# Planned durations of DMAs and of one VectorE add in a list-scheduled attention and int8 layer

## The chip, the cores and the metric

The kernel runs on the 8 cores of one Trainium2 chip. Each core takes two of the 16 sequences and works alone; nothing is exchanged between cores. The metric is the device time of the slowest core, in microseconds (us), lower is better.

## The reference, cut to what matters

```python
x = x + LN(attn(LN(x)))           # x: 16 x 2048 x 1024, f32
x = x + LN(ffn(LN(x)))

# attn: 16 heads of 64, decay linear attention
q = elu(x @ Wq) + 1;  k = elu(x @ Wk) + 1;  v = x @ Wv
a = sigmoid(x @ Wa + ba + 2)      # one decay per head and token
S = a * S + k v^T;  z = a * z + k
out = (q S) / (q z + eps);  return out @ Wo

# ffn: int8 quantised matmul with a 1024 x 1024 matrix
lhs_scale = absmax(lhs, row) / 127;  rhs_scale = absmax(rhs, column) / 127
return (round(lhs / lhs_scale) @ round(rhs / rhs_scale)) * lhs_scale * rhs_scale
```

## The kernel before

A core has 4096 tokens, cut into 32 chunks of 128 tokens (16 of each of its two sequences, taken in turn). Chunks go in pairs, one chunk of each sequence, so there are 16 pairs. The weights stay in SBUF all along.

`front(tc)` handles one chunk up to the scan. Its row sums (L519, L522) and its normalised rows `xn` (L528) are made on ScalarE; `xn` is turned by a transposing DMA on SP into `xnf` (L533, estimate on L537); TensorE makes the decay logits (L543) and the three projections in halves of 512 columns (L597); ScalarE and VectorE make elu + 1 of q and k (L607 to L642, with the two adds of L622 and L642 on VectorE); v gets its weights on VectorE (L702, L707); k is turned by a second transposing DMA (L713) and q by TensorE (L724) with copies at L741 to L748.

`tail_pair(m)` takes a pair to its end. For each of its two chunks `scan_chunk` makes the masked scores (L773, L780), the state products (L799 to L813), the numerators (L825 to L836) and the quotient `otok` (L867); `wo_chunk` turns `otok` by a DMA (L885) and multiplies by Wo (L893), and ScalarE evacuates it (L911, L915). For the pair together come the second normalisation and residual add (L949, L955), the store of x2 to `y`, the load of the x tiles of the pair after next into the freed slots, row maxima and minima (L996, L999), quantisation (L1049 to L1064), a transposing DMA of `ql` (L1071), the int8-valued product (L1079), its evacuation (L1094, L1115), the last normalisation (L1136) and an accumulating DMA into `y` from GpSimd's queue (L1143). `ln_pair` (L1164 to L1177) makes the small statistics.

The order in which an engine does all this isn't the order of the program text. Each call of `S.op` only notes an operation: its engine, what it reads and writes, and an estimated duration `est` in ns (400 where none is given). `Sched.schedule` then plans all operations of the core at once. It works out for each operation `cp`, the longest chain of estimates from it to the end, with `LAT = 320.5` added wherever a chain changes engines, and then gives one operation after another to the engine that can start earliest; among the operations that are ready on it, the one with the largest `cp` goes first. A DMA takes its queue for `min(est, 1600)` and its data is counted as there after `est`. The result is one fixed order for each engine and each DMA queue (SP and POOL), written out with semaphore waits. At run time every engine keeps to its order and waits where the operand isn't there. The core of that planner:

```python
busy = min(nd["est"], DMA_ISSUE) if nd["dma"] else nd["est"]
eng_clock[e] = start + busy
finish[i] = start + nd["est"]
...
v = finish[p] + (LAT if self.nodes[p]["eng"] != nsc["eng"] else 0.0)
```

A pair in steady state issues 16 DMAs: on SP two each of the transposes into `xnf`, `kfm`, `ofm` and `qlf`, two stores of x2 and two half loads of x; on POOL two half loads of x and two accumulating stores.

The text of the estimates sums up as follows for one pair (with 400 where no estimate stands). VectorE: 2 x 8.58 us in `front`, 2 x 8.19 us in `scan_chunk` and 24.67 us in the rest of `tail_pair`, 58.2 us. TensorE: 2 x 14.2 + 2 x 5.2 + 14.4 = 53.2 us. ScalarE: 2 x 14.88 + 2 x 1.2 + 2 x 2.3 + 16.1 = 52.9 us.

Of the kernel before, what the change touches and what calls it, by code (L numbers as in the profile page):

```python
# [210 lines left out]
def build_program(nseq, spc, debug_tc=None):  # L211
# [115 lines left out]

    def dma(q, out, in_, reads=(), writes=()):
        S.op(q, lambda e, o=out, i=in_: e.dma_start(out=o, in_=i),
             reads=reads, writes=writes, dma=True, est=2550)  # L330

    assert nseq == 2

# [19 lines left out]
    for nm, hb in (("Wq", wq_h), ("Wk", wk_h), ("Wv", wv_h)):  # L353
# [4 lines left out]
            writes=[nm + "h"])  # L358
# [7 lines left out]
    for pf in range(2):  # L366
# [3 lines left out]
            writes=["vz_ones%s" % s])  # L370
    S.op("pool", lambda e: e.memset(sb["zeros16"][:, :], 0.0), writes=["zeros16"])
    for pf in range(2):
        s = str(pf)
        S.op("pool", lambda e, s=s: e.memset(sb["qAB" + s][:, :], 0.0),
             writes=["qAB%s_pad" % s])
    for i, v in ((0, LN_EPS), (1, -1.0), (2, -0.5), (3, 1.0)):
        S.op("pool", lambda e, i=i, v=v: e.memset(sb["cst"][:, i:i + 1], v),
             writes=["cst%d" % i])
    S.op("dve", lambda e: e.tensor_scalar_add(sb["ba2"][:, :], sb["ba2"][:, :], A_SHIFT),
         reads=["ba2"], writes=["ba2"])  # L380
    for ld in range(KC):
# [3 lines left out]
            writes=[buf])  # L385
        if ld == 0:
            S.op("dve", lambda e, buf=buf: e.tensor_copy(
                sb["o_f"][:, :], sb[buf][:, :]),
                reads=[buf], writes=["qt_f"])
            S.op("dve", lambda e, buf=buf: e.tensor_copy(  # L390
                sb["x2d"][:, 1024:2048], sb[buf][:, :]),
                reads=[buf], writes=["x2_1"])
        else:
            S.op("dve", lambda e, buf=buf: e.tensor_tensor(
                sb["o_f"][:, :], sb["o_f"][:, :], sb[buf][:, :], OP.max),
                reads=["qt_f", buf], writes=["qt_f"])
# [3 lines left out]
                reads=["x2_1", buf], writes=["x2_1"])  # L400
    S.op("dve", lambda e: e.tensor_scalar_mul(sb["x2d"][:, 1024:2048], sb["x2d"][:, 1024:2048], -1.0),
         reads=["x2_1"], writes=["x2_1"])
    S.op("dve", lambda e: e.tensor_tensor(
        sb["o_f"][:, :], sb["o_f"][:, :], sb["x2d"][:, 1024:2048], OP.max),
        reads=["qt_f", "x2_1"], writes=["qt_f"])
    S.op("dve", lambda e: e.tensor_copy(sb["sqj"][:, :], sb["o_f"][:, :]),
         reads=["qt_f"], writes=["sqj"])
    for c in range(KC):
# [4 lines left out]
            reads=["sqj", "idb"], writes=["pb%d" % (c // 4)])  # L413
    for c in range(KC):
# [5 lines left out]
        reads=["rsT8"], writes=["rsT8"])  # L420
# [10 lines left out]
    for half in range(2):  # L431
        S.op("dve", lambda e, half=half: e.tensor_copy(
            sb["x2d"][0:1, 0:1024][:, half * 512:(half + 1) * 512], pb[2 + half][0:1, :]),
            reads=["pb%d" % (2 + half)], writes=["x2_0" if half else "x2_1"])
    for half in range(2):
# [3 lines left out]
            reads=["x2_0", "x2_1", "ones1"], writes=["pb%d" % (4 + half)])  # L439
    for half in range(2):  # L440
        S.op("dve", lambda e, half=half: e.tensor_copy(
            sb["wrep"][:, half * 512:(half + 1) * 512], pb[4 + half][:, :]),
            reads=["pb%d" % (4 + half)], writes=["wrep" if half else "wrep_h0"])
    S.op("dve", lambda e: e.reciprocal(sb["fn"][:, :], sb["wrep"][:, :]),
         reads=["wrep", "wrep_h0"], writes=["fn"])

    for c in range(KC):
# [5 lines left out]
            writes=[breg])  # L453
        S.op("dve", lambda e, bap=bap: e.tensor_tensor(
            sb["o_f"][:, :], bap, sb["fn"][:, :], OP.mult),
            reads=[breg, "fn"], writes=["qt_f"])
        S.op("dve", lambda e: e.tensor_scalar_add(
            sb["o_f"][:, :], sb["o_f"][:, :], 0.5),
            reads=["qt_f"], writes=["qt_f"])
        S.op("act", lambda e: e.activation(sb["qi"][:, :], sb["o_f"][:, :], AF.Copy),  # L460
             reads=["qt_f"], writes=["qi"])
        S.op("dve", lambda e: e.tensor_tensor(
            sb["gq"][:, :], sb["qi"][:, :], sb["o_f"][:, :], OP.is_gt),
            reads=["qi", "qt_f"], writes=["gq"], est=1180)
# [3 lines left out]
            reads=["gq", "qi"], writes=["QR_c%d" % c])  # L468
    for c in range(KC):
# [4 lines left out]
            reads=["QR_c%d" % c, "wrep", "wrep_h0"], writes=["QR_c%d" % c],  # L474
            est=1180)
# [34 lines left out]
    def front(tc):  # L510
# [10 lines left out]
            reads=xs_reg, writes=["sqj", sum1_reg], est=1100)  # L521
        S.op("act", lambda e, xs=xs, a=ssq1_ap, s=s: e.activation(  # L522
            sb["sqj"][:, :], xs[:, :], AF.Square, accum_out=a),
            reads=xs_reg, writes=["sqj", ssq1_reg], est=1100)
# [5 lines left out]
            reads=xs_reg + [rstd1_reg, bias1_reg], writes=["xn" + s], est=1100)  # L530
# [3 lines left out]
            out=sb["xnf" + s].rearrange("p (c t) -> p c t", t=CK),  # L534
            in_=sb["xn" + s][:, :], transpose=True),
            reads=["xn" + s], writes=["xnf%s_h0" % s, "xnf" + s],
            dma=True, est=2550)  # L537
        xnf_regs = ["xnf" + s, "xnf%s_h0" % s]

        def em_a(e, s=s):  # L540
# [65 lines left out]
        def elu_evac_k(dst):  # L606
            S.op("act", lambda e: e.activation(  # L607
                sb["e_sb"][:, 0:512], pb[2][:, :], AF.Exp),
                reads=["pb2"], writes=["e_h0"], est=680)
            S.op("act", lambda e: e.activation(  # L610
                sb["r_sb"][:, 512:1024], pb[3][:, :], AF.Relu),
                reads=["pb3"], writes=["r_sb"], est=680)
            S.op("act", lambda e: e.activation(
                sb["e_sb"][:, 512:1024], pb[3][:, :], AF.Exp),
                reads=["pb3"], writes=["e_sb"], est=680)
            S.op("act", lambda e: e.activation(
                sb["r_sb"][:, 0:512], pb[2][:, :], AF.Relu),
                reads=["pb2"], writes=["r_h0"], est=680)
            S.op("dve", lambda e, dst=dst: e.tensor_scalar_min(
                sb[dst][:, :], sb["e_sb"][:, :], 1.0),  # L620
                reads=["e_sb", "e_h0"], writes=[dst], est=340)
            S.op("dve", lambda e, dst=dst: e.tensor_add(  # L622
                sb[dst][:, :], sb[dst][:, :], sb["r_sb"][:, :]),
                reads=[dst, "r_sb", "r_h0"], writes=[dst], est=620)

        def elu_evac(dst):
            S.op("act", lambda e: e.activation(
                sb["e_sb"][:, 0:512], pb[0][:, :], AF.Exp),
                reads=["pb0"], writes=["e_h0"], est=680)
            S.op("act", lambda e: e.activation(  # L630
                sb["r_sb"][:, 512:1024], pb[1][:, :], AF.Relu),
                reads=["pb1"], writes=["r_sb"], est=680)
            S.op("act", lambda e: e.activation(  # L633
                sb["e_sb"][:, 512:1024], pb[1][:, :], AF.Exp),
                reads=["pb1"], writes=["e_sb"], est=680)
            S.op("act", lambda e: e.activation(
                sb["r_sb"][:, 0:512], pb[0][:, :], AF.Relu),
                reads=["pb0"], writes=["r_h0"], est=680)
            S.op("dve", lambda e, dst=dst: e.tensor_scalar_min(
                sb[dst][:, :], sb["e_sb"][:, :], 1.0),  # L640
                reads=["e_sb", "e_h0"], writes=[dst], est=340)
            S.op("dve", lambda e, dst=dst: e.tensor_add(  # L642
                sb[dst][:, :], sb[dst][:, :], sb["r_sb"][:, :]),
                reads=[dst, "r_sb", "r_h0"], writes=[dst], est=620)

        proj_group("Wq", 0, 0)
        proj_group("Wq", 1, 1)
# [14 lines left out]
        def em_rm(e, s=s):  # L662
            last = None
            for j in range(3):
# [5 lines left out]
             writes=["pb7"])  # L670
# [4 lines left out]
        def em_pr(e, s=s):  # L675
# [38 lines left out]
            out=sb["kfm" + s].rearrange("p (c t) -> p c t", t=CK),  # L714
            in_=sb["ktok" + s][:, :], transpose=True),
            reads=["ktok" + s], writes=["kfm%s_h0" % s, "kfm" + s],
            dma=True, est=2550)
        for srcn, dst in (("qpre", "q"),):
            for half in range(2):
                def em_t(e, srcn=srcn, half=half, s=s):  # L720
# [162 lines left out]
    def wo_chunk(j, tc, ot_regs, sq_cols, sum_cols):  # L883
        banks = (4, 5) if j == 0 else (2, 3)
        S.op("sync", lambda e: e.dma_start(  # L885
            out=sb["ofm"].rearrange("p (c t) -> p c t", t=CK),
            in_=sb["otok"][:, :], transpose=True),
            reads=ot_regs, writes=["ofm_h0", "ofm"], dma=True, est=2550)

        def em_wo(e, c0, c1, bank_i):  # L890
            last = None
            for kc in range(KC):
                last = e.matmul(pb[bank_i][:, 0:c1 - c0],  # L893
                                sb["ofm"][:, kc * 128:(kc + 1) * 128],
                                sb["Wo"][:, kc * 1025 + c0:kc * 1025 + c1],
                                start=(kc == 0), stop=(kc == KC - 1))
            return last
        S.op("pe", lambda e: em_wo(e, 0, 512, banks[0]),
             reads=["ofm", "ofm_h0", "Wo", "Woh"], writes=["pb%d" % banks[0]],
             est=1800)  # L900
        S.op("pe", lambda e: em_wo(e, 512, 1024, banks[1]),
             reads=["ofm", "ofm_h0", "Wo", "Woh"], writes=["pb%d" % banks[1]],
             est=1800)

        dst = sb["o_f"] if j == 0 else sb["ffn_f"][:, 0:D]
        rg = ("of_h0", "of_h1") if j == 0 else ("ofb_h0", "ofb_h1")
        ex = ["qt_f"] if j == 0 else ["ffn0_h0", "ffn0_h1"]
        sm0, sm0_reg = sum_cols
        sq0, sq0_reg = sq_cols
        pbsrc = pbs[banks[0] // 2]  # L910
        S.op("act", lambda e, dst=dst, a=sm0, pbsrc=pbsrc: e.activation(  # L911
            dst[:, :], pbsrc[:, :], AF.Copy, accum_out=a),
            reads=["pb%d" % banks[0], "pb%d" % banks[1]],
            writes=[rg[0], rg[1], sm0_reg] + ex, est=1150)
        S.op("act", lambda e, a=sq0, dst=dst: e.activation(  # L915
            sb["sqk"][:, :], dst[:, :], AF.Square, accum_out=a),
            reads=[rg[0], rg[1]], writes=["sqk", sq0_reg], est=1150)
        return (dst, [rg[0], rg[1]])

    def tail_pair(m):  # L920
# [125 lines left out]
        for col in range(2):  # L1046
# [24 lines left out]
            S.op("sync", lambda e, qln=qln, qfn=qfn: e.dma_start(  # L1071
                out=sb[qfn].rearrange("p (c t) -> p c t", t=CK),
                in_=sb[qln][:, :], transpose=True),
                reads=[qln], writes=[qfn + "_h0", qfn], dma=True, est=2550)

            def em_ffn(e, c0, c1, bank_i, qfn):
                last = None
# [52 lines left out]
        for col in range(2):  # L1130
            fbuf = sb["fn"] if col == 0 else sb["o_n"]
            fregs = ("fn_h0", "fn") if col == 0 else ("fnB_h0", "fnB")
            fex = [] if col == 0 else ["o_n"]
            src_ap, src_regs = facc_banks[col]
            S.op("act", lambda e, i=src_ap, col=col, fbuf=fbuf,
                 b4=bias4p, s4=sc4pair: e.activation(  # L1136
                fbuf[:, :], i[:, :],
                AF.Identity, bias=b4[:, col:col + 1],
                scale=s4[:, col:col + 1]),
                reads=src_regs + ln4_regs + sc4_regs,  # L1140
                writes=[fregs[0], fregs[1]] + fex, est=1150)
            r0 = row0(a + col)
            S.op("pool", lambda e, r0=r0, fbuf=fbuf: e.dma_start(  # L1143
                out=y_h[r0:r0 + CK, :], in_=fbuf[:, :], accum_op=OP.add),
                reads=[fregs[0], fregs[1], "yh%d" % (a + col)],
                writes=["yh%d" % (a + col)], dma=True, est=2550)

    def ln_pair(tag, sum2, ssq2, sum_regs, ssq_regs, n=D):
        m2_ap = [stc(tag + "_m_a"), stc(tag + "_m_b")]
# [104 lines left out]
```

How the kernel before makes its waits and increments, by code:

```python
        def run(eng):  # L176
            seen = {}
            for i in order[ename]:
                nd = nodes[i]
                sem, mycnt, step = info[i]
                waits = {}
                if nd["dma"] and mycnt > 16:
                    waits[sem] = mycnt - 16
                for p in nd["preds"]:
                    psem, pcnt, _ = info[p]
                    if psem == "pe" and ename == "pe":
                        continue
                    if waits.get(psem, 0) < pcnt:
                        waits[psem] = pcnt
                for s_, c_ in waits.items():
                    if c_ > seen.get(s_, 0):
                        seen[s_] = c_
                        eng.wait_ge(sems[s_], c_)
                nd["emit"](eng).then_inc(sems[sem], step)
            for s_, c_ in extra_final.get(ename, []):
                eng.wait_ge(sems[s_], cnt[s_] if c_ is None else c_)
```

## Time and profile before

| what | us |
|---|---|
| median of two runs | 1175.51 |
| the two runs | 1138.41 and 1212.61 |
| profiled execution, time | 1136.73 |
| profiled execution, span of the slowest core (core 0) | 1135.2 |
| spans of the eight cores | 1127.2 to 1135.2 |
| TensorE busy / VectorE busy / ScalarE busy in that span | 825.9 / 776.0 / 706.4 |

The span runs from the first to the last instruction of a core. Busy times are sums of instruction times on one engine; matmuls are pipelined and their ends are modelled, so TensorE's figure is not TensorE at its peak. The profile also gives, for each wait, what released it, and a chain of work followed back from the last instruction.

### The profile page before, as it was taken

How to read it: one execution, taken by the hardware profiler on the slowest of the kernel's cores; microseconds unless marked ns; L12 is line 12 of the kernel's file. 1: busy time of each engine (PE TensorE's matmuls, PEld its weight loads, DVE VectorE, ACT ScalarE, POOL GpSimd, SP SyncE). 2: the span in 40 equal slices, each digit the busy share in tenths (PEclk: the TensorE clock that was granted, in tenths of full speed). 3: DMA queues.
4: the chain of work that ended last, by engine and by line, in shares of the span. 5: the costliest groups of instructions: out<-in, count | busy, mean ns of one | idle time of the engine just before them, and what ended most of it. 6: DMA issues, size and time to landing. Idle time of an engine off the chain costs nothing.

```text
span 1135.2 us, 18914 instructions; the slowest of 8 cores (1127.2 to 1135.2 us)
## 1 busy us (share of the span) xinstructions
PE 825.9 (73%) x5532; PEld 423.1 (37%) x5532; DVE 776.0 (68%) x1820; ACT 706.4 (62%) x1417; POOL 61.1 (5%) x94
## 2 busy tenths in 40 slices
PE   0017866978878787978797978878797879697812
PEld 0003433444444434443344444444444444344300
DVE  3447898677775858685858676585858585868550
ACT  0036437685858585868577585858685857667332
POOL 1200000000000010001000000001000100000000
PEclk9968888998989898989798999989898989898856
DMA  9995213443446262355344443626253624434232
GB/s 199 208 160 103 61 20 93 69 109 59 113 71 130 39 146 41 91 96 99 80 64 106 65 117 54 128 44 143 39 125 62 129 49 75 102 57 88 49 77 38
DMA packets 159723, 102.16 MB, mean 90 GB/s; under 512 B 138883, under 2 KB 139142, under 8 KB 159622
## 3 DMA queue, kind: packets, MB, share of 16 engines
q1 hardware_dynamic: 146038, 63.17, 25.5%
q0 software_dynamic: 13584, 37.79, 18.6%
q8 instruction: 46, 0.75, 0.3%
q14 instruction: 55, 0.45, 0.1%
HBM read 42.24 MB, written 33.55 MB: 67 GB/s over the span
## 4 chain that ended last, share of the span: by engine, by line
PE 41%; DMA 16%; DVE 16%; ACT 13%; issue 12%; POOL 1%; DVEq 0%; ACTq 0%; SPq 0%; POOLq 0%
PE pbs L597 17%; PE pbs L1079 8%; PE pbs L893 6%; DMA s_xs<-x 6%; DMA s_xnf<-s_xn 4%; DVE s_scm L780 3%; DVE s_vz L702 2%; ACT s_xn L528 2%; PE pbs L773 2%; PE pb L679 2%; DMA s_Wq<-wq 2%; DVE s_ql L1064 2%; ACT s_x2d L949 1%; DMA s_Wv<-wv 1%; PE pb L682 1%
## 5 line engine op out<-in xcount | busy, mean ns | idle before, releaser
L597 PE MATMUL pbs<-s_Wq,s_xnf 128*128 128x512 bf16 x512 | 126.7, 401 | 65.9 <-DMA s_xnf<-s_xn 37.0
L1079 PE MATMUL pbs<-s_QR,s_qlf 128*128 128x512 bf16 x512 | 145.9, 436 | 28.9 <-DMA s_qlf<-s_ql 26.5
L597 PE MATMUL pbs<-s_Wv,s_xnf 128*128 128x512 bf16 x512 | 123.6, 391 | 12.3 <-ACT s_e_sb L633 12.2
L893 PE MATMUL pbs<-s_Wo,s_ofm 128*128 128x512 bf16 x512 | 121.1, 388 | 4.0 <-DMA s_ofm<-s_otok 3.9
L597 PE MATMUL pbs<-s_Wk,s_xnf 128*128 128x512 bf16 x512 | 119.0, 379 | 2.8 <-DMA s_xnf<-s_xn 1.3
L780 DVE TENSOR_TENSOR s_scm<-pbs,s_mask 128x512 bf16<-128x512 f32 x128 | 82.0, 681 | 42.2 <-PE pbs L773 42.0
L597 PEld LDWEIGHTS pbs<-s_Wq,s_xnf 128*128 128x128 bf16 x512 | 49.4, 101 | 136.5 <-issue 90.3
L1079 PEld LDWEIGHTS pbs<-s_QR,s_qlf 128*128 128x128 bf16 x512 | 51.8, 108 | 95.4 <-issue 60.0
L1094 ACT ACTIVATE s_ffn_f<-pbs 128x1024 f32<-128x1024 f32 x32 | 32.7, 1023 | 86.9 <-PE pbs L1079 86.9
L597 PEld LDWEIGHTS pbs<-s_Wv,s_xnf 128*128 128x128 bf16 x512 | 48.8, 100 | 72.0 <-issue 20.4
L893 PEld LDWEIGHTS pbs<-s_Wo,s_ofm 128*128 128x128 bf16 x512 | 48.1, 99 | 63.1 <-issue 12.1
L597 PEld LDWEIGHTS pbs<-s_Wk,s_xnf 128*128 128x128 bf16 x512 | 49.1, 98 | 60.3 <-issue 4.1
L799 PE MATMUL pbs<-s_vz,s_ktok 128*64 128x65 bf16 x256 | 17.3, 211 | 63.1 <-DVE s_vz L707 57.7
L519 ACT ACTIVATE s_sqj<-s_xs 128x1024 bf16<-128x1024 f32 x32 | 33.8, 1056 | 37.1 <-DMA s_xs<-x 36.3
L955 DVE TENSOR_TENSOR s_x2d<-s_x2d,s_xs 128x1024 f32<-128x1024 f32 x32 | 38.1, 1218 | 23.4 <-ACT s_x2d L949 21.0
L1143 POOL DMA_DIRECT2D y<-s_fn x16 | 14.0, 877 | 679.9 <-ACT s_fn L1136 362.8
L825 PE MATMUL pbs<-s_vz,s_scm 128*128 128x65 bf16 x192 | 34.6, 216 | 18.3 <-DVE s_Pg_all L813 17.8
L773 PE MATMUL pbs<-s_qAB,s_kfm 128*128 128x256 bf16 x256 | 42.6, 282 | 5.9 <-DVE s_scm L780 3.0
L657 ACT ACTIVATE s_vz<-pbs 128x1024 bf16<-128x1024 f32 x32 | 32.6, 1020 | 20.7 <-PE pbs L597 19.3
L1056 ACT ACTIVATE s_qi<-s_wrep 128x1024 int8<-128x1024 f32 x32 | 33.7, 1052 | 14.0 <-DVE s_wrep L1049 13.9
L528 ACT ACTIVATE s_xn<-s_xs,s_st 128x1024 bf16<-128x1024 f32 x32 | 39.5, 1236 | 3.7 <-DVE s_st L502 2.6
L1060 DVE TENSOR_TENSOR s_gq<-s_qi,s_wrep 128x1024 bf16<-128x1024 int8 x32 | 38.9, 1215 | 4.3 <-ACT s_qi L1056 3.1
(172 smaller groups left out, 1929.8 us busy)
## 6 DMA issues: line engine op xcount, KB each, us to landing
y<-s_x2d SPq DMA_DIRECT2D x32, 512.0 KB, 5.6
s_xs<-x SPq DMA_DIRECT2D x32, 256.0 KB, 5.7
s_xs<-x POOLq DMA_DIRECT2D x32, 256.0 KB, 6.4
y<-s_fn POOLq DMA_DIRECT2D x16, 512.0 KB, 5.5
y<-s_o_n POOLq DMA_DIRECT2D x16, 512.0 KB, 6.0
s_o_n<-rhs SPq DMA_DIRECT2D x8, 512.0 KB, 6.9
s_fn<-rhs POOLq DMA_DIRECT2D x4, 512.0 KB, 8.8
s_Wq<-wq POOLq DMA_DIRECT2D x2, 1024.0 KB, 17.6
```

Of the source, the lines that this page charges most:

```text
L519: S.op("act", lambda e, xs=xs, a=sum1_ap: e.activation(sb["sqj"][:, :], xs[:, :], AF.Copy, accum_out=a), reads=xs_reg, writes=["sqj", sum1 ...
L528: S.op("act", lambda e, xs=xs, s=s, b=bias1_ap, sc=rstd1_ap: e.activation(sb["xn" + s][:, :], xs[:, :], AF.Identity, bias=b, scale=sc), re ...
L597: last = e.matmul(pb[bank_i][:, :], sb["xnf" + s][:, kc * 128:(kc + 1) * 128], sb[W][:, kc * 1024 + gidx * 512:kc * 1024 + (gidx + 1) * 51 ...
L773: return e.matmul(pb[bank][:, col:col + 256], sb["kfm" + s][:, p * 128:(p + 1) * 128], sb["qAB" + s][:, p * 256:(p + 1) * 256], start=True ...
L780: S.op("dve", lambda e, b=b, q=q: e.tensor_tensor(sb["scm"][:, q * 512:(q + 1) * 512], pb[2 + b][:, :], sb["mask4"][:, :], OP.mult), reads ...
L825: e.matmul(pb[nm_bank][:, col:col + 65], sb["scm"][:, p * 256:p * 256 + 128], sb["vz" + s][:, hA * 65:(hA + 1) * 65], start=True, stop=False)
L893: last = e.matmul(pb[bank_i][:, 0:c1 - c0], sb["ofm"][:, kc * 128:(kc + 1) * 128], sb["Wo"][:, kc * 1025 + c0:kc * 1025 + c1], start=(kc = ...
L955: S.op("dve", lambda e, xs_=xs_, col=col: e.tensor_add(sb["x2d"][:, col * D:(col + 1) * D], sb["x2d"][:, col * D:(col + 1) * D], xs_[:, :] ...
L1056: S.op("act", lambda e, qtb=qtb: e.activation(sb["qi"][:, :], qtb[:, :], AF.Copy), reads=["qtb"], writes=["qi"], est=1150)
L1060: S.op("dve", lambda e, qtb=qtb, gqn=gqn: e.tensor_tensor(sb[gqn][:, :], sb["qi"][:, :], qtb[:, :], OP.is_gt), reads=["qi", "qtb"], writes ...
L1079: last = e.matmul(pb[bank_i][:, 0:c1 - c0], sb[qfn][:, kc * 128:(kc + 1) * 128], sb["QR"][:, kc * 1025 + c0:kc * 1025 + c1], start=(kc == ...
L1094: S.op("act", lambda e, col=col, a=sfh0: e.activation(sb["ffn_f"][:, col * D:(col + 1) * D], pbs[2][:, :], AF.Copy, accum_out=a), reads=[" ...
```

## The change

Only numbers of the planner change. Every DMA's `est` goes from 2550 to 2500 at its six places (the helper `dma` of all plain loads and stores, the transposes into `xnf`, `kfm`, `ofm` and `qlf`/`qlf2`, and the accumulating store), and the `est` of the two adds that end elu + 1 (`qpre`, `ktok`) goes from 620 to 625. Operations, operands, tiles and queues stay as they are; only the planner's order can come out otherwise.

```diff
     def dma(q, out, in_, reads=(), writes=()):
         S.op(q, lambda e, o=out, i=in_: e.dma_start(out=o, in_=i),
-             reads=reads, writes=writes, dma=True, est=2550)
+             reads=reads, writes=writes, dma=True, est=2500)
...
             reads=["xn" + s], writes=["xnf%s_h0" % s, "xnf" + s],
-            dma=True, est=2550)
+            dma=True, est=2500)
...
             S.op("dve", lambda e, dst=dst: e.tensor_add(
                 sb[dst][:, :], sb[dst][:, :], sb["r_sb"][:, :]),
-                reads=[dst, "r_sb", "r_h0"], writes=[dst], est=620)
+                reads=[dst, "r_sb", "r_h0"], writes=[dst], est=625)
...
             reads=["ktok" + s], writes=["kfm%s_h0" % s, "kfm" + s],
-            dma=True, est=2550)
+            dma=True, est=2500)
...
-            reads=ot_regs, writes=["ofm_h0", "ofm"], dma=True, est=2550)
+            reads=ot_regs, writes=["ofm_h0", "ofm"], dma=True, est=2500)
...
-                reads=[qln], writes=[qfn + "_h0", qfn], dma=True, est=2550)
+                reads=[qln], writes=[qfn + "_h0", qfn], dma=True, est=2500)
...
                 reads=[fregs[0], fregs[1], "yh%d" % (a + col)],
-                writes=["yh%d" % (a + col)], dma=True, est=2550)
+                writes=["yh%d" % (a + col)], dma=True, est=2500)
```

The add stands twice (in `elu_evac` and `elu_evac_k`), with the same edit.

## Rows read from the trace of the kernel before

**Rows 1.** The page's head and busy time of each engine, slowest core.

```profile
span 1135.2 us, 18914 instructions; the slowest of 8 cores (1127.2 to 1135.2 us)
...
PE 825.9 (73%) x5532; PEld 423.1 (37%) x5532; DVE 776.0 (68%) x1820; ACT 706.4 (62%) x1417; POOL 61.1 (5%) x94
```

**Rows 2.** The page's chain that ended last, by engine.

```profile
PE 41%; DMA 16%; DVE 16%; ACT 13%; issue 12%; POOL 1%; DVEq 0%; ACTq 0%; SPq 0%; POOLq 0%
```

**Rows 3.** Busy time by stretch, cut at each pair's L996: stretch, length, engines.

```profile
core 0: us, PE busy (x) PEld busy (x) DVE busy (x) ACT busy (x) POOL busy (x), PEclk, DMA share, GB/s
0.00:177.94 177.94, 78.52 (x452) 37.56 (x453) 111.78 (x178) 58.22 (x110) 18.15 (x35) 0.87 0.63 121
...
354.48:419.25 64.77, 49.90 (x357) 26.23 (x355) 46.36 (x118) 46.66 (x95) 3.46 (x5) 0.95 0.39 83
419.25:478.65 59.40, 51.25 (x348) 26.56 (x346) 43.56 (x110) 41.38 (x86) 1.63 (x3) 0.91 0.35 79
478.65:536.40 57.75, 48.01 (x334) 25.23 (x332) 41.46 (x102) 42.54 (x85) 3.51 (x5) 0.94 0.54 100
536.40:601.80 65.40, 51.44 (x355) 26.69 (x354) 46.28 (x117) 46.49 (x95) 3.46 (x5) 0.90 0.42 85
601.80:662.06 60.26, 50.84 (x348) 26.48 (x346) 43.75 (x109) 41.32 (x86) 1.65 (x3) 0.92 0.38 77
662.06:719.62 57.56, 48.26 (x334) 25.05 (x332) 41.48 (x102) 42.37 (x85) 3.50 (x5) 0.94 0.55 100
719.62:786.60 66.98, 51.95 (x356) 26.54 (x354) 46.29 (x117) 46.42 (x95) 3.44 (x5) 0.90 0.39 82
786.60:844.35 57.75, 48.68 (x346) 25.82 (x345) 43.56 (x109) 41.48 (x87) 1.64 (x3) 0.94 0.36 82
844.35:903.19 58.84, 49.87 (x336) 25.62 (x335) 41.28 (x102) 42.55 (x85) 3.55 (x5) 0.91 0.50 98
...
1087.33:1135.20 47.87, 10.15 (x32) 3.63 (x32) 13.89 (x28) 11.53 (x18) 1.68 (x2) 0.61 0.23 51
```

**Rows 4.** Waits of the whole span: who waited for whom, us, times, longest.

```profile
ACT s_ffn_f L1094 <- PE pbs L1079: 86.9, 32, 8.0
...
PE pbs L799 <- DVE s_vz L707: 57.7, 19, 4.3
...
PE pbs L597 <- DMA s_xnf<-s_xn: 38.4, 13, 22.4
ACT s_sqj L519 <- DMA s_xs<-x: 36.3, 15, 11.8
...
PE pbs L1079 <- DMA s_qlf<-s_ql: 26.5, 5, 24.0
```

**Rows 5.** DMA issues by line: out<-in, queue, count, median us to landing.

```profile
s_xs<-x SPq DMA_DIRECT2D x32, 256.0 KB, 5.7
s_xs<-x POOLq DMA_DIRECT2D x32, 256.0 KB, 6.4
...
s_kfm<-s_ktok SPq DMA_TRANSPOSE x32, 3.1
```

**Rows 6.** Groups of instructions by line: count, busy us, mean ns.

```profile
L893 PE MATMUL pbs<-s_Wo,s_ofm 128*128 128x512 bf16 x512 | 121.1, 388 | 4.0 <-DMA s_ofm<-s_otok 3.9
...
L996 DVE TENSOR_REDUCE s_st<-s_x2d 128x2 f32<-128x2048 f32 x16 | 36.6, 2286 | 0.8
...
L642 DVE TENSOR_TENSOR s_qpre<-s_qpre,s_r_sb 128x1024 bf16<-128x1024 bf16 x32 | 22.1, 692 | 3.0 <-ACT s_rep L688 0.2 <-DVE s_qpre L639 0.2
...
L622 DVE TENSOR_TENSOR s_ktok<-s_ktok,s_r_sb 128x1024 bf16<-128x1024 bf16 x32 | 22.0, 688 | 1.3
...
L1164 DVE TENSOR_SCALAR s_st<-s_st 128x2 f32<-128x2 f32 x48 | 8.0, 166 | 33.7 <-ACT s_ffn_f L911 33.1
```

**Rows 7.** The chain in order of time in a long pair: start, us, what.

```profile
718.00 7.34 DMA s_xs<-x
725.41 1.16 ACT s_sqj L519 x2
...
764.39 2.78 DMA s_xnf<-s_xn
767.16 0.14 issue
767.30 3.61 PE pbs L597 x16
```

More of the change, by code:

```diff
@@ L643, in elu_evac @@
                 sb[dst][:, :], sb[dst][:, :], sb["r_sb"][:, :]),
-                reads=[dst, "r_sb", "r_h0"], writes=[dst], est=620)
+                reads=[dst, "r_sb", "r_h0"], writes=[dst], est=625)
         proj_group("Wq", 0, 0)
```

## The prediction

> **What bounds the kernel now.** I read the page's head first. No engine is full: TensorE is busy for 825.9 us of 1135.2 (73%), VectorE for 776.0 and ScalarE for 706.4 [rows 1]. The page's chain that ended last says the same from the other side: TensorE holds 41% of it, and the rest is shared by DMA 16%, VectorE 16%, ScalarE 13% and issue 12% [rows 2]. So the time is set by the order in which engines hand work to each other, and the order is the one thing that this change can touch.
>
> Next the span by stretch, cut where each pair starts its row maxima (L996, 16 instances, first at 177.94 us, last at 1087.33) [rows 3]. The start takes 177.9 us, fifteen pair intervals take 909.4, the end 47.9; together 1135.2. The reader should look down the column of lengths from 354.48 on: 64.8, 59.4, 57.8, then 65.4, 60.3, 57.6, then 67.0, 57.8, 58.8. The VectorE counts go with them: 118, 110, 102, then 117, 109, 102, then 117, 109, 102. The plan isn't one pattern per pair but a cycle of three pairs, and it repeats almost to the instruction. The nine intervals take 903.19 - 354.48 = 548.71 us, 60.97 a pair, in which VectorE works 394.02 / 9 = 43.78 and therefore idles 17.19.
>
> The lengths can't be compared raw, since a long interval also holds more work. Length less VectorE's busy time is the fairer measure of how well an interval is packed: long kind 18.41, 19.12, 20.69, mean 19.41; the other six 15.84, 16.29, 16.51, 16.08, 14.19, 17.56, mean 16.08 [rows 3]. Even the worst kind and the best differ by only some 3 us a pair. These figures price a different order below.
>
> Last the waits [rows 4]. The large ones are between engines: 86.9 us for the int8 product, 57.7 for the weighted v. Waits for transfers are small once the edges are set aside: TensorE waits 38.4 us for `xnf`, of which 22.4 is one wait in the start, leaving 16.0 in 12; and 26.5 for `qlf`, of which 24.0 is one wait, leaving 2.5 in 4; and 3.9 for `ofm` [rows 6]. ScalarE waits 36.3 us in 15 for the x tiles.
>
> **The change part by part.** *What it removes, adds or moves on the chip directly: nothing.* Not one instruction or byte changes, so the direct term is 0. A DMA still takes its queue for 1600 in the plan, since min(2500, 1600) is min(2550, 1600); SP and POOL are as free in the plan as before. What changes is when the data of a DMA counts as there, 50 ns sooner, and the `cp` of all that lies before a DMA, lower by 50 for each DMA on its longest chain.
>
> *The add, 620 to 625.* Four of them a pair, so VectorE's planned load goes from 58.21 to 58.23 us a pair. Measured they take 688 and 692 ns [rows 6], so the plan comes nearer by 5 of some 70 ns. It is worth nothing by itself; I take 0.
>
> *The DMAs, 2550 to 2500.* A transpose takes 3.1 us to its landing as the trace shows for `kfm`, an x half 5.7 us on SP and 6.4 on POOL [rows 5]. The plan was too hopeful by 0.55 us and by 3.2 to 3.9 us, and gets more so by 0.05. If each of the 128 transposes were waited for, and each had its reader set 50 ns too early, this would cost 128 x 0.05 = 6.4 us; only 12 + 4 + 2 = 18 of them are waited for now, beside the edges [rows 4, 6], so 18 x 0.05 = 0.9 us. I take +1 or less: nothing visible. Below nothing there is no direct gain, since a plan with shorter DMAs makes none of them land sooner.
>
> *Does the order change at all?* VectorE has 329 / 3 = 109.7 operations a pair [rows 3] in a planned 58.2 us, one every 0.53 us. Each of the 16 DMAs of a pair frees its readers 50 ns earlier, and this matters where another decision lies inside those 50 ns: 16 x 0.05 / 0.53 = 1.5 places a pair, beside those where two `cp` values change their order. Over a cycle of three pairs that is 4 to 5 places. So some order changes almost surely, and as the plan is repeated, what changes once comes back in each cycle.
>
> *What a changed place costs.* The trace of before holds no other order of the same pair, so this is bounded from its rows. Two neighbours that change places delay one by the length of the other: from 0.17 us (L1164) through 0.69 (the adds) to 2.29 (L996) on VectorE, and on TensorE a column half of a projection, eight matmuls, 1.8 us (16 take 3.61) [rows 6, 7]. Most such delays vanish in the 17.2 us of idle time a pair; where that cover is gone, as on the last chain of the pair, it is paid in full. One exposed swap of 0.7 us a pair is 15 x 0.7 = 10 us, two are 21. The sign is open: the plan has one order of each kind and I have no reason why the swap should hurt more often than help.
>
> From the other side: if the new plan were made of intervals of the long kind only, idle time would rise by 19.41 - 17.19 = 2.22 a pair, 15 x 2.22 = +33 us; of the other kinds only, 16.08 - 17.19 = -1.11, -17 us. The best single interval (14.19) throughout would be -45, the worst (20.69) +53 [rows 3]. I take 0 for the size, since it lies between the bounds and the sum of small swaps of either sign goes there, and keep -45 and +53 for the range.
>
> *A sign of steadiness.* From 354 us on the kernel repeats its three-pair cycle to within one or two VectorE instructions through three rounds, although the start of the run is quite different [rows 3]. A plan that falls back into the same cycle from another start may well fall into a near relative of it with numbers changed by 2%.
>
> **Sum.** Span 1135.2 + 0 (adds) + 1 (DMAs) + 0 (order) = 1136.2; outside the span the profiled execution has 1136.7 - 1135.2 = 1.5, so 1137.7. That is a difference of 1 that nobody can measure, and I say 1137. The two other runs of before are 1138.4 and 1212.6, and their median 1175.5 stands 38.8 above the profiled execution; the sum is meant for executions like the profiled one.
>
> **Rivals.** *Slower: the early readers.* The new cycle sets readers ahead of data that isn't there, and the engine, which keeps its order, stands before them with other work behind. It begins where the reader of an x tile (L519, load 7.34 us in the chain) or of `xnf` (2.78 us, then 3.6 us of projections) stands on the last chain, as in the long interval [rows 7]. Beside it: the Trainium skill, DMA: Bandwidth & Descriptors, "Rules for kernel authors", says to issue a DMA early and to wait for it as late as can be, which is against any estimate made shorter; that ScalarE has 15 waits for x agrees with it. The price is that of a cycle with long intervals only, +33 us, 1170. It decides from 1.5 us a pair on (1.5 x 15 = 23 us, 2%). For it: every DMA is already underestimated. Against: 50 ns is a small part of that error, and of ScalarE's 36.3 us of waiting for x one wait alone is 11.8 [rows 4].
>
> *Faster: a better-packed cycle.* The new plan drops the long interval, and the pairs idle between 16.08 and 14.19 us: -17 to -45, middle -31, 1106. For it: the last round shows an interval of 14.19 in the same work (109 operations) that took 16.51 a round earlier. Against: to gain 2% the whole cycle must be better than two of its three present kinds.
>
> *No change of order.* Then it is the same kernel, 1136.7. With 4 to 5 places expected in each cycle I give this 3 in 100.
>
> *Neither plan matters: the clock.* The granted clock moves between 0.90 and 0.95 from interval to interval [rows 3]; 0.02 of 49 us busy is 1 us a pair, 15 us at most, and stays within 2%. It is part of the forecast's spread.
>
> **How the numbers follow.** A difference of 2% (23 us) is about what a measurement of this kernel can tell from no change. Forecast (order changes, cycle about as good, 1137): 0.53. No change of order: 0.03. Faster rival (1106): 0.23. Slower rival (1170): 0.21. Faster by over 2%: 0.23; within 2%: 0.56; slower: 0.21. The range leaves out a tenth on each side: down to 1100, between the middle (-31) and the bound (-45) of the faster rival, and up to 1176, a little past the slower one (+33) and short of +53. The likeliest case has 1114 to 1160 as its own range.
>
> **What would show it.** Right: intervals between the L996 that repeat in a cycle with a mean of 60 to 62 us; the same counts of instructions; transposes at 3.1 us; VectorE idle about 17 us a pair; start near 178 and end near 48 us. The slower rival would show as more and longer waits of ScalarE L519 for x or of TensorE L597 for `xnf`, and as more intervals of 64 to 67 us. The faster one would show intervals with less than 16 us of idle. The forecast is wrong if the mean interval leaves 59.4 to 62.5 us, or if the start, with its loads of weights, moves by over 20 us.

## The result and the profile after

The changed kernel takes 1147.4 us (median), the kernel before 1138.4. The ratio is 1.0071, with a 95% interval from 1.0051 to 1.0091: slower by 0.7%, which is small but clear of the noise. The kernels have a second, slower state that comes in some executions whatever the kernel; ratios are taken without those executions, medians with them, so a ratio need not equal the quotient of two medians. The profiled execution of the changed kernel has a span of 1144.6 us on its slowest core. The page's head and its chain by engine:

```profile
span 1144.6 us, 18923 instructions; the slowest of 8 cores (1125.4 to 1144.6 us)
...
PE 37%; DMA 20%; DVE 15%; issue 13%; ACT 12%; POOL 0%; DVEq 0%; ACTq 0%; SPq 0%; POOLq 0%
```

Against [rows 2], TensorE's share of the chain has gone from 41% to 37% and that of the DMAs from 16% to 20%; the transpose into `ofm` alone holds 5% of it. The stretches between the starts of L996, slowest core, columns as in [rows 3]:

```profile
0.00:177.60 177.60, 78.84 (x452) 37.99 (x453) 112.41 (x179) 58.51 (x110) 18.30 (x35) 0.95 0.65 121
...
360.92:423.04 62.12, 49.40 (x346) 25.61 (x345) 43.63 (x109) 43.93 (x90) 2.88 (x5) 0.95 0.40 84
423.04:483.14 60.10, 49.00 (x346) 25.48 (x345) 43.58 (x109) 43.83 (x90) 2.87 (x5) 0.94 0.42 88
483.14:543.75 60.61, 49.58 (x346) 25.61 (x345) 43.64 (x109) 43.74 (x89) 2.87 (x5) 0.94 0.40 87
...
790.17:855.53 65.36, 53.53 (x346) 26.72 (x345) 43.63 (x109) 43.84 (x90) 2.71 (x4) 0.87 0.38 82
...
1096.35:1144.60 48.25, 9.86 (x32) 3.63 (x32) 13.89 (x28) 11.53 (x18) 1.69 (x2) 0.61 0.23 51
```

The reader should look at the counts. Before, VectorE's counts went 118, 110, 102 and round again; now each interval shown has 109, 43.6 us of VectorE and 346 matmuls. The planner has left its cycle of three pairs for a cycle of one pair. A few intervals are longer with the same work, as the one of 65.4 us, in which the granted clock was 0.87.

The waits (who waited for whom, us in total, times, longest):

```profile
ACT s_ffn_f L1094 <- PE pbs L1079: 67.4, 32, 7.7
...
ACT s_sqj L519 <- DMA s_xs<-x: 43.8, 17, 14.6
...
ACT s_ffn_f L911 <- PE pbs L893: 40.9, 15, 9.8
...
PE pbs L597 <- DMA s_xnf<-s_xn: 38.6, 13, 22.1
...
PE pbs L1079 <- DMA s_qlf<-s_ql: 25.2, 5, 24.2
```

Of the waits named in [rows 4], those for the int8 product, `xnf` and `qlf` are lower or the same (67.4 for 86.9 us, 38.6 for 38.4, 25.2 for 26.5); ScalarE's for the x tiles is longer (43.8 for 36.3). A new one stands at the product with Wo: the page's group of L893 gives 24.8 us of idle time before it, 17.4 of them for the transpose, where [rows 6] had 4.0 and 3.9:

```profile
L893 PE MATMUL pbs<-s_Wo,s_ofm 128*128 128x512 bf16 x512 | 125.2, 394 | 24.8 <-DMA s_ofm<-s_otok 17.4
```

The issues of DMAs (out<-in, queue, count, median us to landing) say why:

```profile
s_kfm<-s_ktok SPq DMA_TRANSPOSE x32, 3.1
s_ofm<-s_otok SPq DMA_TRANSPOSE x32, 6.1
```

The transpose of `otok` moves the same bytes as that of `ktok`, and took the same 3.1 us in before:

```profile
s_ofm<-s_otok SPq DMA_TRANSPOSE x32, 3.1
```

Now its median is 6.1 us. That median needs care: here the profile tells the landing of only 16 of the 32 transposes, and 14 of these are the second of their pair. By the semaphore updates in the trace the first of each pair still lands in 3.1 to 3.3 us, and the second, from the third pair on, in 5.3 to 8.2. In order of time, one pair of the changed kernel (start, duration on its queue or engine), first ScalarE, then POOL's queue, then SP's:

```profile
767.99 1.22 ACT L1136 ACTIVATE s_fn<-s_ffn_f,s_st 128x1024 f32<-128x1024 f32 x1
769.12 1.00 ACT L911 ACTIVATE s_o_f<-pbs 128x1024 f32<-128x1024 f32 x1
...
769.78 0.88 POOL L1143 DMA_DIRECT2D y<-s_fn  x1 [39.23 <-ACT s_fn L1136]
...
770.13 1.22 SPq L885 DMA_TRANSPOSE s_ofm<-s_otok  x1
```

and the chain at the same place (start, us, what):

```profile
770.13 6.41 DMA s_ofm<-s_otok
776.53 0.25 issue
776.78 3.62 PE pbs L893 x16
```

The accumulating store of 512 KB goes out 0.35 us ahead of the transpose, and the transpose then needs 6.41 us; the product with Wo starts on its landing. In the kernel before, the same three read as follows, with the product's start beside them:

```profile
701.40 1.02 ACT L911 ACTIVATE s_o_f<-pbs 128x1024 f32<-128x1024 f32 x1 [1.60 <-PE pbs L893]
...
706.16 1.23 ACT L1136 ACTIVATE s_fn<-s_ffn_f,s_st 128x1024 f32<-128x1024 f32 x1
...
701.39 1.24 SPq L885 DMA_TRANSPOSE s_ofm<-s_otok  x1
...
704.71 3.62 PE L893 MATMUL pbs<-s_Wo,s_ofm 128*128 128x512 bf16 x16
...
707.96 0.86 POOL L1143 DMA_DIRECT2D y<-s_fn  x1 [31.96 <-ACT s_fn L1136]
```

There ScalarE evacuates the first Wo product (L911) before it makes `fn` (L1136), so the store goes out 6.57 us after the transpose, when that has landed. In the new order L1136 stands directly before this L911; in the three kinds of pair of the old cycle it stands two, three or eight instructions behind it. Here is the distance from the issue of each pair's second `ofm` transpose to that of the nearest y<-s_fn store, read off the two queues of the profiled core, all pairs from the second on:

| kernel | distance, us (negative: the store goes first) |
|---|---|
| before | +3.7 to +6.6 |
| changed | second pair +4.1, third -1.7, all others -0.04 to -0.42 |

So the change did not lengthen any wait directly. It moved a ScalarE instruction ahead of another, and with it a store onto a transpose. Since hundreds of other places change too, which of them brings the two together is not shown; that they meet is.

The kernel before isn't free of such meetings either. In every third pair its store goes out 0.6 us ahead of the transpose into `xnf` of the pair's second chunk, which then lands in 6.0 to 6.9 us (by the semaphore updates). But the waits of TensorE for `xnf` come to the same 38 us in both kernels: what a lengthened transfer costs depends on when its reader is due.

### The profile page after: what moved, and what is told of

Same layout as the page of the kernel before. It is cut to its first block, busy times and chain, and to the rows that moved or that the text cites. A ratio compares the mean times of both kernels' runs of the same rounds, so it can differ in the third digit from the quotient of the medians.

```text
span 1144.6 us, 18923 instructions; the slowest of 8 cores (1125.4 to 1144.6 us)
## 1 busy us (share of the span) xinstructions
PE 824.2 (72%) x5532; PEld 418.7 (37%) x5532; DVE 774.1 (68%) x1820; ACT 711.6 (62%) x1417; POOL 61.4 (5%) x94
## 4 chain that ended last, share of the span: by engine, by line
PE 37%; DMA 20%; DVE 15%; issue 13%; ACT 12%; POOL 0%; DVEq 0%; ACTq 0%; SPq 0%; POOLq 0%
PE pbs L597 14%; PE pbs L1079 10%; DMA s_xs<-x 7%; PE pbs L893 6%; DMA s_ofm<-s_otok 5%; DMA s_qlf<-s_ql 3%; DVE s_scm L780 2%; DMA s_xnf<-s_xn 2%; DVE s_ql L1064 2%; PE pbs L773 2%; DMA s_Wq<-wq 2%; DMA s_Wv<-wv 1%; DVE s_otok L867 1%; DVE s_x2d L955 1%; PE pb L679 1%
## 5 line engine op out<-in xcount | busy, mean ns | idle before, releaser
L1079 PE MATMUL pbs<-s_QR,s_qlf 128*128 128x512 bf16 x512 | 143.1, 430 | 28.1 <-DMA s_qlf<-s_ql 25.2
L597 PE MATMUL pbs<-s_Wq,s_xnf 128*128 128x512 bf16 x512 | 124.1, 397 | 48.4 <-DMA s_xnf<-s_xn 38.6
L893 PE MATMUL pbs<-s_Wo,s_ofm 128*128 128x512 bf16 x512 | 125.2, 394 | 24.8 <-DMA s_ofm<-s_otok 17.4
L893 PEld LDWEIGHTS pbs<-s_Wo,s_ofm 128*128 128x128 bf16 x512 | 48.3, 100 | 86.5 <-issue 40.5
L1094 ACT ACTIVATE s_ffn_f<-pbs 128x1024 f32<-128x1024 f32 x32 | 32.8, 1024 | 67.4 <-PE pbs L1079 67.4
L519 ACT ACTIVATE s_sqj<-s_xs 128x1024 bf16<-128x1024 f32 x32 | 33.8, 1058 | 44.1 <-DMA s_xs<-x 43.8
L1164 DVE TENSOR_SCALAR s_st<-s_st 128x2 f32<-128x2 f32 x48 | 8.0, 166 | 56.4 <-ACT s_ffn_f L911 54.7
L799 PEld LDWEIGHTS pbs<-s_vz,s_ktok 128*64 128x64 bf16 x256 | 13.3, 128 | 86.8 <-issue 86.8
```

The costliest lines, as they stand in the source:

```text
L519: S.op("act", lambda e, xs=xs, a=sum1_ap: e.activation(sb["sqj"][:, :], xs[:, :], AF.Copy, accum_out=a), reads=xs_reg, writes=["sqj", sum1 ...
L597: last = e.matmul(pb[bank_i][:, :], sb["xnf" + s][:, kc * 128:(kc + 1) * 128], sb[W][:, kc * 1024 + gidx * 512:kc * 1024 + (gidx + 1) * 51 ...
L799: e.matmul(pb[bank][0:64, col:col + 65], sb["ktok" + s][:, hA * 64:(hA + 1) * 64], sb["vz" + s][:, hA * 65:(hA + 1) * 65], start=True, sto ...
L893: last = e.matmul(pb[bank_i][:, 0:c1 - c0], sb["ofm"][:, kc * 128:(kc + 1) * 128], sb["Wo"][:, kc * 1025 + c0:kc * 1025 + c1], start=(kc = ...
L1079: last = e.matmul(pb[bank_i][:, 0:c1 - c0], sb[qfn][:, kc * 128:(kc + 1) * 128], sb["QR"][:, kc * 1025 + c0:kc * 1025 + c1], start=(kc == ...
L1094: S.op("act", lambda e, col=col, a=sfh0: e.activation(sb["ffn_f"][:, col * D:(col + 1) * D], pbs[2][:, :], AF.Copy, accum_out=a), reads=[" ...
```

## The experiments

The order of the instructions shows first which edit does what. Built one at a time: the estimate of the plain loads and stores, of the accumulating store, of the `kfm` transpose, and of the add in `elu_evac_k` (L622) each leave all five orders exactly as before. The add in `elu_evac` (L642) alone changes 4 places on each of TensorE, VectorE and ScalarE. The estimate of `qlf` alone gives the one-pair cycle and the new SP and POOL orders; that of `ofm` alone a cycle of two pairs; that of `xnf` alone another cycle of three pairs with SP and POOL as before. Of these single edits only those of `qlf` and `xnf` were run. All edits together change 526 of 1292 places on TensorE, 1033 of 1820 on VectorE, 789 of 1192 on ScalarE, 16 of 208 on SP and 12 of 90 on POOL.

**e1: only the `qlf` estimate.**

```diff
-                reads=[qln], writes=[qfn + "_h0", qfn], dma=True, est=2550)
+                reads=[qln], writes=[qfn + "_h0", qfn], dma=True, est=2500)
```

> Only the transpose into qlf/qlf2 is planned with 2500; all other estimates stay as before. The planner then also falls into a cycle of one pair (the order of SP and POOL is that of the changed kernel). Theory A (the new one-pair cycle is about as fast as the old three-pair one, 60.6 against 61.1 us a pair, but its second ofm transpose lands in 6.1 instead of 3.1 us because the y<-s_fn store is issued just ahead of it, and its first three intervals are 3.7 us longer): this kernel shows all of that, ofm at 6 us, intervals equal, and lies 0.3 to 1.2% above before. Theory B (the adds or the other DMAs matter): it is as before, within 0.3%.

It took 1160.0 us, ratio to before 1.0206 (1.0170 to 1.0242). One number out of eight makes the kernel slower by 2.1%, three times as much as all eight. The `ofm` transpose lands in 6.3 us, the store goes out 0.03 to 0.42 us ahead of it in nearly every pair, TensorE waits 17.9 us for it. The mechanism of theory A is there; its size was set too low, and e6 below shows that this order of the engines is worse than the changed kernel's besides.

**e2: only the `xnf` estimate.**

```diff
             reads=["xn" + s], writes=["xnf%s_h0" % s, "xnf" + s],
-            dma=True, est=2550)
+            dma=True, est=2500)
```

> Only the transpose into xnf is planned with 2500. SP and POOL keep the order of before; TensorE, VectorE and ScalarE get another order in a cycle of three pairs. Theory A (what costs is where the store meets the ofm transpose): ofm lands in 3.1 us, long and short intervals alternate as before, within 0.4% of before. Theory B (any departure from the old order costs): 0.5% or more slower.

1137.4 us, ratio 0.9998 (0.9977 to 1.0018). Three engines run another order, the store stays 3.55 to 7.44 us behind the transpose, `ofm` lands in 3.1 us, and the time doesn't move. This departure from the old order costs nothing, so that theory B, by which any does, falls.

**e3: the changed kernel, the store held back.** The planner's orders are left as they are; after planning, one edge is added, so that POOL waits for the landing of the next pair's second `ofm` transpose before it issues y<-s_fn (`S.yst` and `S.ofm` hold the numbers of the stores and transposes by chunk). Lines of the kernel move down by up to 7.

```diff
     nodes = S.nodes
+    for tc, nid in S.yst.items():
+        if tc % 2 == 0 and tc + 3 in S.ofm:
+            nodes[nid]["preds"].add(S.ofm[tc + 3])
```

> The changed kernel in its own order, with one edge more: the y<-s_fn store of a pair waits until the second ofm transpose of the next pair has landed. Theory A (contention of the 512 KB accumulating store with the transpose holds back Wo): ofm lands in 3.1 us, TensorE's wait for ofm falls from 17 us to under 4, and the time falls by 1.5 to 3 us a pair, 20 to 40 us in all, to 1105 to 1125. Theory C (the wait is covered by something else that ends at the same time, such as xnf or ScalarE): ofm lands in 3.1 us but the time falls by less than 8 us. Theory D (ofm is slow for another reason, such as the xnf transpose ahead of it): ofm still lands in 6 us.

1121.8 us, ratio 0.9846 (0.9820 to 0.9872). Divided by the changed kernel's 1.0071 that is 0.978, or 25 us less. Its DMA issues (median us to landing):

```profile
s_ofm<-s_otok SPq DMA_TRANSPOSE x32, 3.1
```

SP's queue, TensorE and POOL's queue in one pair:

```profile
574.29 1.23 SPq L891 DMA_TRANSPOSE s_ofm<-s_otok  x1
...
577.88 1.90 PE L602 MATMUL pbs<-s_Wv,s_xnf 128*128 128x512 bf16 x8
579.62 3.62 PE L899 MATMUL pbs<-s_Wo,s_ofm 128*128 128x512 bf16 x15
...
578.00 0.88 POOL L1150 DMA_DIRECT2D y<-s_fn  x1 [42.85 <-DMA s_ofm<-s_otok]
```

The store now leaves 3.7 us after the transpose. All landings of `ofm` are at 3.1 us. Of TensorE's 11 waits for it one is left, in the last pair (4.8 us, where theory A had under 4 in all), and ScalarE's wait for the product with Wo falls from 40.9 to 16.2 us:

```profile
PE pbs L899 <- DMA s_ofm<-s_otok: 4.8, 1, 4.8
ACT s_ffn_f L917 <- PE pbs L899: 16.2, 15, 6.2
```

Theories C and D fall. This version beats both kernels, and no engine's wait for that store is among its listed waits.

The rows also say what the delay costs. TensorE runs the same work in both kernels while the transpose is under way (all of Wq, the decay logits, half of Wv). In e3 that keeps it busy until 5.3 us after the issue of the transpose (median), so that 2.2 us of delay would cost nothing; in the changed kernel the product starts after 6.3 us. Summed over the pairs from the third on, the product starts 21 us earlier in e3, which is most of the 25. The store does not go out into an empty stretch: it now stands 2 us ahead of the next transpose into `xnf`, which lands in 4.0 to 5.6 us where the changed kernel had 3.0 to 4.6, and TensorE's wait for `xnf` stays at 38.5 us.

**e4: the order of the start.** The first three intervals of the changed kernel take 180.9 us (mean over the cores of the profiled execution), those of before 177.2. Here the transposes of the first two pairs are planned with 2550.

```diff
-            dma=True, est=2500)
+            dma=True, est=2500 if tc >= 4 else 2550)
```

(and so for `ofm`, and for `qlf` with `m >= 2`)

> The changed kernel's estimates, but the transposes of the first two pairs are planned with 2550: the first pairs keep an order near before's, the rest runs in the new one-pair cycle. If the longer first three intervals (180.9 against 177.2 us, mean over the cores) come from the new order there, the time falls by 2 to 4 us against the changed kernel and stays 4 to 6 above before. If the spread of the cores in the new cycle is what makes the slowest core late, it stays at 0.4 to 0.7% above before.

1146.6 us, ratio 1.0063 (1.0040 to 1.0086), as the changed kernel. The first three intervals still take 180.4 us. The first meeting comes only one pair later than in the changed kernel. In e3 the three take 177.2 with the changed kernel's own order: their excess was the store too. The other thought, that only the spread between cores had grown, falls with the means. Over all cores the mean span is 1128.0 us in before, 1135.9 in the changed kernel, 1134.2 in e4 and 1110.9 in e3; the slowest core stands 8.0, 8.9, 9.3 and 7.8 us above it. Of the 8.8 us by which the slowest core is later, 7.9 are in every core.

**e5: the edge of e3 in the kernel before.** The same three added lines.

> The kernel before in its own order, with the same added edge as e3: y<-s_fn waits for the second ofm transpose of the next pair. In before the store already goes out 4 to 7 us after that transpose, which lands in 3.1 us. Theory A (only the meeting of the two costs): nothing changes, within 0.3% of before. Theory E (a late store helps in any order, for example by leaving the DMA engines to the loads of x): faster by 1% or more as e3.

1138.0 us, ratio 1.0017 (0.9994 to 1.0039). Where the store and the transpose into `ofm` don't meet, the edge is worth nothing. Theory E falls.

**e6: the edge of e3 in e1.**

> The kernel of e1 (only the qlf estimate at 2500, 1160 us, ofm in 6.3 us) with the edge of e3. Theory A: ofm lands in 3.1 us and the time falls by as much as in the changed kernel, 20 to 30 us, to 1130 to 1140. If e1 is slow by its own order of the compute engines besides, it stays above e3's 1121.8; if the meeting was all, it comes to within 5 us of it.

1127.2 us, ratio 0.9915 (0.9898 to 0.9933), against 1.0206 without the edge: 33 us less. `ofm` lands in 3.1 us. It stays above e3 (0.9915 against 0.9846, 8 us), so the two orders differ by that much of their own; without the edge they differed by 1.0206 to 1.0071, 15 us.

**e7: half the store.** The y<-s_fn store of each pair's first chunk carries 512 of its 1024 columns; the last sum is left out for the others.

```diff
+            w = D // 2 if col == 0 else D
-                out=y_h[r0:r0 + CK, :], in_=fbuf[:, :], accum_op=OP.add),
+                out=y_h[r0:r0 + CK, 0:w], in_=fbuf[:, 0:w], accum_op=OP.add),
```

> The changed kernel in its own order, no edge, but the y<-s_fn store carries only columns 0 to 511 (256 instead of 512 KB), so the last sum is left out for the other half of the columns of every first chunk of a pair. Theory A with contention in proportion to the bytes: ofm lands in about 4.5 instead of 6.1 us and the time falls by 8 to 15 us, to 1130 to 1140. If a fixed latency of the accumulating store is what holds the transpose, ofm stays at 6 us and so does the time (1144 to 1148).

The landing times follow the bytes:

```profile
y<-s_fn POOLq DMA_DIRECT2D x16, 256.0 KB, 4.3
...
s_ofm<-s_otok SPq DMA_TRANSPOSE x32, 4.8
```

The store still goes first, by about 0.3 us. With 512 KB the transpose took 6.1 us, with 256 KB 4.8, with none in flight 3.1. But the time came to 1121.4 us (ratio 0.9874, 0.9858 to 0.9889), lower than the 1130 to 1140 expected. Against the changed kernel's 1.0071 that is 22 of the 25 us that e3 gives, though only 1.3 of the 3.0 us of delay are gone. The slack found in e3 explains it:

```profile
698.69 1.22 SPq L885 DMA_TRANSPOSE s_ofm<-s_otok  x1
...
703.98 3.62 PE L893 MATMUL pbs<-s_Wo,s_ofm 128*128 128x512 bf16 x16
```

The product starts 5.3 us after the issue, as in e3, because TensorE isn't free sooner and a landing after 4.8 us is early enough. Of TensorE's wait for `ofm`, 17.4 us in 11 in the changed kernel, 8.3 in 4 are left, 6.8 of them in the last pair. The store also moves 4 MB less over the run, which no run separates; but the intervals after the third take 59.4 us in e7 and 59.5 in e3 (means over the cores), so that little is left for it to explain.

**e8: the durations of the DMAs and adds as measured.** Since the planner works on wrong durations, what do better ones bring? All other estimates stay, and they are off as well: VectorE's add up to 58.2 us a pair where it is busy for 43.8.

```diff
-             reads=reads, writes=writes, dma=True, est=2550)
+             reads=reads, writes=writes, dma=True, est=6000)
```

(transposes 3100, the accumulating store 5700, the adds 690)

> The planner's numbers set to what the trace shows: transposes 3100, plain loads and stores 6000, the accumulating store 5700, the adds 690. No edge. The order is again a cycle of one pair, a third one. Theory F (a more truthful plan gives a better order): 1% or more faster than before. Theory A (the plan does not know of transfers that meet, so truth in the durations settles nothing): anything from -2 to +2%, decided by whether an ofm transpose lands in 3.1 us or in 6; if it lands in 3.1, faster than before.

1200.6 us, ratio 1.0577 (1.0551 to 1.0604). The kernel with these more truthful numbers is by far the slowest, outside both expectations. From the third pair on its store goes out 0.04 to 0.83 us before the transpose. The median of `ofm` on the page is 3.1 us all the same, and hides the meeting: the 16 landings that the profile tells here are those of the first transpose of each pair. The chain shows one of the second ones:

```profile
1064.81 6.55 DMA s_ofm<-s_otok
```

By the semaphore updates the second ones land in 5.8 to 7.6 us from the third pair on. The start takes 188.3 us instead of 173.6 (mean over cores; TensorE works 3.6 us in the first 90, where in before it worked 6.5), and a later interval takes 64 us in the mean.

**e9: the edge of e3 in e8.**

> The kernel of e8 (durations as measured, 1200 us) with the edge of e3. If the meeting of y<-s_fn and the second ofm transpose is part of its loss (there the store goes out 0.3 us ahead too, at 675.51 against 675.83), the time falls by 10 to 25 us to 1175 to 1190; the rest, above all the start of 188 instead of 173 us and 62 to 64 us a pair, stays. If the order of the compute engines is all of it, it stays at 1195 to 1205.

1176.3 us, ratio 1.0243 (1.0203 to 1.0283). From 1.0577 that is 3.2% or some 38 us for the meeting alone; the medians differ by 24 only, but come from chips on which the kernel before took 1136.0 and 1145.6. What stays, 2.4%, is the start (189.9 us, 16 more than in before) and the orders themselves; they were not taken apart further.

## Why the prediction was right or wrong

The forecast was no measurable change, 1137 us with 1100 to 1176. The time, 1147.4, lies within the range and within 2%, but the kernel moved by 0.71% with an interval clear of zero, and the forecast had given it no direction. It was wrong. Its sign on the intervals did not show that: their mean is 61.25 us, inside the 59.4 to 62.5 that it allowed. (Its sum, 1136.2 + 1.5, gives 1137.7, not the 1137 that it then took; nothing hangs on that.)

*What bounds the kernel.* Right, and it carried over: no engine is full, and the order decides.

*The direct terms.* Right. Nothing on the chip changed by the edit itself; e2 changes an estimate and is at 0.9998. The add of `elu_evac_k` and three of the estimates of DMAs change no order at all.

*Does the order change.* Right in kind, far off in size: it counted 1.5 changed places a pair, and 1033 of VectorE's 1820 places changed, since the plan falls into another cycle. The text also took each DMA of a pair as a chance to change a place, while three of the six estimates of DMAs did nothing in any of 16 pairs, and a single one, `qlf`, gives the new cycle by itself.

*The sign of steadiness.* Wrong. The old cycle looked like one into which the plan falls back. 2% off one duration put it into cycles of one, two or three pairs. That a plan returns to its cycle from another start doesn't say that it survives other durations.

*What a changed place costs.* This is the step that failed. It priced a swap by the length of the neighbour on the same engine and kept every transfer at its measured landing time, so that the term "order" of the sum came out as 0; "transposes at 3.1 us" even stood among the signs that the forecast was right. What mattered was where L1136 stands to the transpose of the next pair. The price is not its 1.2 us but a store that then starts 0.04 to 0.42 us before a transpose instead of 3.7 to 6.6 us after it, and lengthens it by 3 us a pair, of which 2.2 us would be covered by other work and the rest is paid. With the edge of e3 set and unset this is worth 25 us.

*The bounds from the intervals.* The size was right for the wrong sum. The new cycle without the meeting is faster by 1.5% (0.9846), -17 us: about what the prediction worked out for a plan of its better intervals only, though the agreement may be chance, as the new intervals hold other work than the old ones and meetings with `xnf` lie in both. The meeting adds 25 and the sum is +8. The term "order, 0" was two terms of opposite sign, -17 and +25. Something like the better packing of the faster rival was there, and was more than paid back.

*The slower rival.* It looked for readers set ahead of their data, at L519 and `xnf`, because every DMA is underestimated. The wait at `xnf` did not move (38.6 for 38.4 us). That at L519 rose (43.8 for 36.3), but it is 40.9 in e3, which is faster than before, so that it isn't what made the difference. And e8, which cures the underestimate of the DMAs, is the slowest kernel of all. The Trainium skill, DMA: Bandwidth & Descriptors, "Rules for kernel authors" (issue early, wait late), did not help here, since the reader had not moved closer to its transfer: the second product with Wo starts 4.1 us after the issue of its transpose in before (median), and 5.3 in e3, which has the changed kernel's order. The transfer had become longer.

*The clock.* Right: not a cause. The mean granted clock over all cores is 0.908 in the changed kernel and 0.905 in before.

## What to carry to other kernels

A planner that knows durations and dependencies but not the shared DMA engines can put two transfers on top of each other in every iteration; after any change of order, compare the landing time of each DMA that stands on the path with its own time before, not only the engines' waits, and issue by issue: a median may cover only some of them, as in e8. Where a long store that nobody waits for starts within a transfer's time of a short one that the next product needs, make the store wait for the short one: one edge was worth 2.2% here, and nothing where they did not meet. Measure the slack of the reader too: a delay below it cost next to nothing (e7). Better numbers for some of the operations are no safe step in such a planner: those of e8 cost 5.8%.

## What the runs showed of the hardware

A transposing DMA of 128 x 1024 bf16, issued from SP, lands in 3.1 us where no store from POOL goes out near it (`ofm` in before and e3). With an accumulating store of 512 KB issued from POOL ahead of it, it takes longer the closer the two are: 4.0 to 5.6 us with some 2 us between them (`xnf` in e3), 5.3 with 1.7, and 5.9 to 8.2 with 0.04 to 0.42 (`ofm` in the changed kernel). With a store of 256 KB and 0.1 to 0.4 us between them it takes 4.5 to 5.8 us (e7). This agrees with the Trainium skill, DMA: Bandwidth & Descriptors, "Issuing engines are not separate DMA queues", by which transfers from all issuing engines run on the same 16 DMA engines and interleave. It isn't peculiar to accumulating stores: nine `kfm` transposes of the changed kernel, issued 3 to 5 us behind three half loads of x and two stores of x2, took 5.3 us (median). That a lead of 0.04 us is enough was not expected.
